# First and fourth attention: rounded upper halves of queries and keys on ScalarE, lower halves on VectorE, both from PSUM

## The chip, the cores and the metric

The kernel runs on one core of one Trainium2 chip. Its time is the device time of one execution in microseconds (us). Engines: TensorE (PE, its weight loads PEld), VectorE (DVE), ScalarE (ACT), GpSimd (POOL), SyncE (SP, which issues nearly all DMAs).

## What is computed

Four layers on x, 16 batches of 112 tokens with 256 features. Each adds a cross-attention with a context of 375 rows a batch, and then a feed-forward part (three mixtures of experts and a dense one). The change concerns the attentions of layer 0 and layer 3, which have 16 heads of 16 features:

```python
qh = (q @ W_q.T + b_q)...;  kh = (k @ W_k.T + b_k)...;  vh = (v @ W_v.T + b_v)...   # q = layernorm(x), k = v = ctx
scores = einsum('bhqd,bhkd->bhqk', qh, kh) / sqrt(16)
scores = where(mask == 0, -inf, scores)          # layer 3: -1e9
x = x + softmax(scores) @ vh ... @ W_o.T + b_o   # layer 3: the same without biases
```

The mask drops the same keys for all heads and queries.

## The kernel before

One program holds the instruction streams of the five engines; they meet at semaphores only. An attention is a list of steps, `Att.steps`, that PE, DVE and ACT each walk in the same order, each taking its own part of a step. The list is made of **slots**, one for each head: 256 for the 16 batches of an attention with 16 heads, plus a tail. In slot g stand, in this order: in slot 5 of a batch the `norm` step of the batch before (DVE: reciprocals of the sums and their spreading, L1146 and L1149); `scores` of head g (PE L918, then the DVE row minimum L1169, which adds the mask and writes the sum to SBUF; ACT's exponential of it, L1217, comes with a later step); `turn` of head g-3 (PE transposes, L935; the copy out of PSUM is DVE's, L1190, for three heads of eight, and ACT's, L1224, for the others), after which ACT takes the exponential of head g; in every fourth slot `pv` (PE L966); in slot 5 a transpose of the reciprocals (PE L871, ACT L1258, DVE L1060, which multiplies them in); and last the slot's "extras", which are the projections.

The projections of batch b+1 are spread over the 16 slots of batch b by `spread`. Each item has a cost; its slot is the first slot of the batch plus 15 times the share of the cost done before it, and never earlier than the item before it. For the output projection `o` of batch b-1 the rule also asks for at least one slot after the item before it, and for slot 7 or later: `max(first + int(done / total * count), earliest, last + (step is o))`. In a steady batch the queries q come in slot 0, key tile k0 in slot 1, k1 in slot 4, o in slot 8, the three value tiles in slots 9, 11 and 13. Two marks of cost 0 stand among the keys: `split` 0 (slot 1, ahead of k0), `split` 1 (slot 4, ahead of the next item) and `split` 2 (slot 7). Projections use PSUM banks 5, 6 and 7 in turn; projection n waits until projection n-3 is read out.

The score matmul of a head is one pass in the F32R format, over 128 rows that stack four 32-row pieces: products of rounded upper and rounding-error lower halves of queries and keys. They are made so: DVE reads the queries from PSUM and multiplies them by a 0/-0.25 pattern, once for each parity of heads (L1076 in layer 0, with bias; L1079 in layer 3), 2 x 224 columns; ACT reads a key tile from PSUM (L1247, L1249); `split` then runs on DVE from SBUF to SBUF: a rounding copy (L1049) and a subtraction (L1051). The halves go to DRAM ("spill", SP L1290 for queries, L1293 for keys) and come back rearranged ("stack": `qS` by four DMAs L1299, `kS` by four DMAs L1303 for each key tile). Scores of slots 0 to 7 need the first key tile's stack, those of slots 8 to 15 the second one's. SP issues in order: query spill, k0 spill, 4 query stacks, 4 k0 stacks, k1 spill, 4 k1 stacks, a context load.

Of the kernel before, what the change touches and what calls it, by code (L numbers as in the profile page):

```python
# [24 lines left out]
F32 = mybir.dt.float32  # L25
# [85 lines left out]
class Att:  # L111
# [4 lines left out]
    def __init__(self, L, sems, before):  # L116
# [30 lines left out]
        if self.stack:  # L147
            self.spilled = sems[f"spilled{L}"]
            self.split = sems[f"split{L}"]
            self.stacked, self.stacked8 = sems[f"stacked{L}"], sems[f"stacked8{L}"]  # L150
# [30 lines left out]

    def proj(self, b):
# [5 lines left out]
        if self.stack:  # L188
            return q + [(("split", b, 0), 0, 0), k[0], (("split", b, 1), 0, 0), k[1], (("split", b, 2), 0, 0)], v
        return ([(("ctx", b), 0, 0)] if self.halves else []) + q + k, v  # L190
# [27 lines left out]
    def steps(self):  # L218
# [7 lines left out]
        def spread(items, first, count):  # L226
# [18 lines left out]
        if H > 1:  # L245
            a, c = self.proj(0)
            ahead = [s for s, _, _ in a + c]
            for b in range(B):
# [214 lines left out]
def build(nc, A):  # L463
    ctx = ExitStack()
    with ctx:
# [8 lines left out]
        sel16 = sb("sel16", [P, 8])  # L474
# [42 lines left out]
        sel2 = sb("sel2", [P, 2])  # L517
# [3 lines left out]
        keys = wflat[:, 0:6 * SKE].rearrange("p (k o t) -> p k o t", k=3, o=2)  # L521
        queries = wflat[:, 6 * SKE:6 * SKE + 12 * S].rearrange("p (k o t) -> p k o t", k=3, o=2)
        STACK = 32
        NSTACK = P // STACK
        STACK_DMAS = [2 * NSTACK * 16, NSTACK * 16]
# [52 lines left out]
        for L in (0, 3):  # L578
            att_sems[f"spilled{L}"] = [sem(f"l{L}a_spilled{k}") for k in range(3)]
            att_sems[f"stacked8{L}"] = [sem(f"l{L}a_stacked8{k}") for k in range(2)]  # L580
            att_sems[f"split{L}"] = sem(f"l{L}a_halves")
            att_sems[f"stacked{L}"] = [sem(f"l{L}a_stacked{k}") for k in range(2)]
        att_sems["halved"] = sem("l2a_halved")
        folded_ps, folded_sb = sem("l1a_folded_psum"), sem("l1a_folded_sbuf")
# [62 lines left out]
        qhalves = nc.dram_tensor("query_halves", (2, 2 * P, 2 * S), F32).ap()  # L647
# [330 lines left out]
        def att_vector(dve, t):  # L978
            L, H, dh, per = t.L, t.H, t.dh, t.per
            n_chain = t.ch0  # L980
            if t.masked:
# [3 lines left out]
                dve.tensor_scalar(maskf[:, :], m[:, :], 0.0, t.a["fill"], ALU.is_equal, ALU.mult)\  # L985
# [27 lines left out]
            if t.stack:  # L1013
                dve.memset(keys[:, 0, :, SK:SKE], 0.0).then_inc(t.chain, 1)
# [23 lines left out]
            def split(b, part):  # L1038

                a = queries if part == 0 else keys[:, :, part - 1:part, :]  # L1040
                if part == 0:
                    freed(dve, t, t.gen_index("q", b, 0))
                else:
                    freed(dve, t, t.gen_index("k", b, part - 1))
                at = b * 6 + part * 2
                if part and b:
                    former, n = (t.stacked8, STACK_DMAS[1]) if part == 2 else (t.stacked, STACK_DMAS[0])
                    dve.wait_ge(former[(b - 1) % 2], n * ((b - 1) // 2 + 1))
                dve.tensor_copy(a[:, 1].bitcast(F32R), a[:, 0]).then_inc(t.split, 1)  # L1049
                dve.wait_ge(t.split, at + 1)  # L1050
                dve.tensor_tensor(a[:, 2].bitcast(F32R), a[:, 0], a[:, 1], ALU.subtract).then_inc(t.split, 1)  # L1051

            def gen(kind, b, o, h, n):
# [10 lines left out]
                if kind in "kn" or (kind == "v" and not t.a["bv"]) or (kind == "q" and H == 1):  # L1064
                    return
                dve.wait_ge(t.gen_ready, t.g0 + n + 1)
                if kind == "q" and t.stack:

                    if b:
                        dve.wait_ge(t.stacked[(b - 1) % 2], STACK_DMAS[0] * ((b - 1) // 2 + 1))  # L1070
                    by_parity = sel2[:, :].unsqueeze(2).broadcast_to([P, 2, S])
                    for j in range(t.NO):
                        out = queries[:, 0, j, :].rearrange("p (e s) -> p e s", e=2)
                        q2 = src[:, j * S:(j + 1) * S].unsqueeze(1).broadcast_to([P, 2, S])
                        if t.a["bq"]:
                            ins = dve.scalar_tensor_tensor(out=out, in0=q2, scalar=biasA[:, 0, j:j + 1],  # L1076
                                                           in1=by_parity, op0=ALU.add, op1=ALU.mult)
                        else:
                            ins = dve.tensor_tensor(out, q2, by_parity, ALU.mult)  # L1079
                elif kind == "q":  # L1080
# [79 lines left out]
            for s in t.plan:  # L1160
                if s[0] == "gen":
                    gen(*s[1:])
                elif s[0] == "scores":
# [19 lines left out]
                elif s[0] == "turn":  # L1183
# [6 lines left out]
                    dve.tensor_copy(pTb(t, g), bank[2 + g % 2][0:KT, 0:NKT * S]).then_inc(t.pt_sbuf[1], 1)  # L1190
                elif s[0] == "ctx":
                    halve_context(s[1])
                elif s[0] == "split":
                    split(s[1], s[2])
# [7 lines left out]
        def att_scalar(act, t):  # L1202
# [29 lines left out]

            def gen(kind, b, o, h, n):
                if kind in "or" or (kind == "q" and H > 1) or (kind == "v" and t.a["bv"]):
                    return
                src = bank[t.banks[n % t.GB]]
                act.wait_ge(t.gen_ready, t.g0 + n + 1)
                if kind == "q":
                    ins = act.activation(qall[:, o, b * S:b * S + TOK], src[:, 0:TOK], ACT.Identity,
                                         bias=folded[:, o:o + 1], scale=-t.a["scale"])  # L1240
                elif kind == "k":
                    out = keys[:, 0, o, 0:SK] if t.stack else kTv(t, b)[:, o, :]
                    if t.stack and b:
                        former, m = (t.stacked8, STACK_DMAS[1]) if o else (t.stacked, STACK_DMAS[0])
                        act.wait_ge(former[(b - 1) % 2], m * ((b - 1) // 2 + 1))
                    if t.a["bk"]:
                        ins = act.activation(out, src[:, 0:SK], ACT.Identity, bias=biasA[:, 1, o:o + 1])  # L1247
                    else:
                        ins = act.activation(out, src[:, 0:SK], ACT.Copy)  # L1249
                elif kind == "v" and t.stack:  # L1250
                    if b == 0 and o == 0:
                        act.wait_ge(padded, 2)
# [25 lines left out]
        def stack_sync(sp, t):  # L1278
# [4 lines left out]
            def batch(b):  # L1283
# [5 lines left out]
                sp.wait_ge(t.split, b * 6 + 2)  # L1289
                sp.dma_start(spill(qhalves), queries[:, 1:3]).then_inc(t.spilled[0], 16)  # L1290
                for o in range(2):
                    sp.wait_ge(t.split, b * 6 + 4 + o * 2)
                    sp.dma_start(spill(khalves[o]), keys[:, 1:3, o:o + 1, :]).then_inc(t.spilled[1 + o], 16)  # L1293
                    if o == 0:
                        if b >= 2:
                            sp.wait_ge(t.scores, t.h0 + (b - 1) * t.H)
                        sp.wait_ge(t.spilled[0], b * 16 + 16)
# [3 lines left out]
                    sp.wait_ge(t.spilled[1 + o], b * 16 + 16)  # L1301
# [860 lines left out]
        def _(pool):  # L2162
            pool.memset(part(V_AT, 2 * VPAD, KT), 0.0).then_inc(padded, 1)
            nc.gpsimd.iota(lanei[:, :], pattern=[[1, P]], base=0, channel_multiplier=0).then_inc(consts, 1)
# [4 lines left out]
            nc.gpsimd.memset(sel16[:, :], -ATT[0]["scale"]).then_inc(consts, 1)  # L2169
# [159 lines left out]
```

## Time and profile before

| what | value |
|---|---|
| median of 3 runs | 2513.31 us (2509.89 to 2515.79) |
| the profiled execution's own time | 2517.43 us |
| its span in the trace | 2515.4 us |
| layer 0 attention, first score to last pv | about 50 to 386 us |
| layer 3 attention, first score to last pv | about 2063 to 2391 us |
| busy over the span | PE 90%, PEld 69%, DVE 50%, ACT 42%, POOL 12% |

A row of the timeline has start, length, engine, line, operation, output<-input, shape and count; in square brackets the engine's idle time just before and who ended it. "mx" is the row minimum that the score needs, bank is PSUM, arena is one large SBUF tile that holds most buffers. In the chain of waits a row has start, length, what. Lines are those of the kernel before.

### The profile page before, as it was taken

Reading aid. Unit: us, or ns where it says so; the run is one execution under the profiler, and the core shown is the slowest. Engines: PE = TensorE matmul, PEld = TensorE weight load, DVE = VectorE, ACT = ScalarE, POOL = GpSimd, SP = SyncE. Lnnn points to the kernel's source line nnn. Section 1 sums busy time; section 2 is a strip of 40 time slices with the busy share of each in tenths; the row PEclk is TensorE's granted clock in tenths of the full one; section 3 lists DMA queues with packets and bytes.
Section 4 is the critical chain, followed back from the end, with each engine's and each line's share of the span. In section 5 each row is a group of like instructions: output and inputs, shape, how many; then the busy total and the mean of one; then the engine's idle time right before and its main releaser. Section 6 shows DMA issues by size and latency. Waiting matters only on the chain.

```text
span 2515.4 us, 44690 instructions
## 1 busy us (share of the span) xinstructions
PE 2254.5 (90%) x15374; PEld 1737.6 (69%) x15374; DVE 1254.1 (50%) x3592; ACT 1048.3 (42%) x2821; POOL 300.1 (12%) x349
## 2 busy tenths in 40 slices
PE   4999998999967899679999999999869949999998
PEld 3777776677746667467777777777547637777755
DVE  5777884222243522544445444454432267777713
ACT  2777772222132122134444444444312227877811
POOL 0000001111151245100000000000024300000020
PEclk8999998999978799889999999999869969999999
DMA  6887875222254212310000000000042168888600
GB/s 187 204 199 198 200 173 238 84 84 86 82 146 153 112 61 72 73 53 10 14 7 17 11 17 7 11 17 1 17 189 65 59 183 203 200 199 201 148 11 22
DMA packets 149433, 252.53 MB, mean 100 GB/s; under 512 B 14736, under 2 KB 124640, under 8 KB 146544
## 3 DMA queue, kind: packets, MB, share of 16 engines
q1 hardware_dynamic: 138560, 220.31, 32.4%
q0 software_dynamic: 10656, 29.37, 3.6%
q8 instruction: 131, 2.15, 0.4%
q14 instruction: 86, 0.70, 0.1%
HBM read 191.04 MB, written 58.59 MB: 99 GB/s over the span
## 4 chain that ended last, share of the span: by engine, by line
PE 76%; DVE 12%; DMA 5%; issue 4%; ACT 1%; SPq 1%; DVEq 0%; POOL 0%; ACTq 0%; POOLq 0%
PE bank L1676 8%; PE bank L935 7%; PE bank L966 6%; PE bank L1709 6%; PE bank L854 5%; PE bank L850 5%; PE bank L1741 5%; PE bank L880 4%; PE bank L923 4%; PE bank L865 3%; PE bank L841 3%; PE bank L1726 3%; PE bank L918 2%; PE bank L2034 2%; PE bank L2020 2%
## 5 line engine op out<-in xcount | busy, mean ns | idle before, releaser
L935 PE MATMUL bank<-ident,arena 112*125 112x112 f32 x2352 | 371.7, 275 | 3.3 <-DVE arena L1190 0.3
L935 PEld LDWEIGHTS bank<-ident,arena 112*125 112x125 f32 x2352 | 338.1, 188 | 46.5 <-issue 12.3
L1217 ACT ACTIVATE arena<-arena,mx 112x375 f32<-112x375 f32 x512 | 308.6, 604 | 116.5 <-DVE mx L1169 115.8
L1169 DVE CUSTOM_DVE_ANT_0 arena<-bank,maskf 112x375 f32<-112x375 f32 x512 | 273.3, 542 | 80.7 <-PE bank L918 79.1
L918 PE MATMUL bank<-kS,qS 128*112 128x376 f32 x512 | 236.4, 462 | 47.1 <-DMA kS<-key_halves 23.5
L1181 DVE TENSOR_REDUCE mx<-bank 112x1 f32<-112x375 f32 x256 | 128.8, 543 | 239.6 <-PE bank L923 239.5
L1676 PE MATMUL bank<-arena 128*128 x532 | 229.9, 555 | 3.4 <-ACT arena L1802 2.7
L1190 DVE COPY arena<-bank 125x336 f32<-125x336 f32 x448 | 214.2, 502 | 33.6 <-PE bank L935 33.6
L1217 ACT ACTIVATE arena<-bank,mx 112x375 f32<-112x375 f32 x272 | 156.0, 575 | 171.5 <-DVE mx L1181 150.1
L966 PE MATMUL bank<-arena 125*32 125x112 f32 (+1 forms) x4608 | 202.5, 265 | 2.9 <-DVE arena L1190 2.9
L966 PEld LDWEIGHTS bank<-arena 125*32 125x32 f32 (+1 forms) x4608 | 144.2, 118 | 85.6 <-issue 67.9
L1320 POOL TENSOR_TENSOR rstd<-newton,root 112x2 f32<-112x2 f32 x32 | 22.7, 709 | 1483.0 <-DVE newton L1125 1482.9
L1224 ACT ACTIVATE arena<-bank 125x336 f32<-125x336 f32 x336 | 147.0, 438 | 58.9 <-PE bank L935 55.9
L1709 PE MATMUL bank<-arena 128*128 (+1 forms) x672 | 167.1, 380 | 0.0
L850 PE MATMUL bank<-ctx_halves,weight_halves 128*128 128x376 f32 x768 | 144.8, 341 | 9.7 <-DVE arena L1082 9.7
L854 PE MATMUL bank<-weight_halves,ctx_halves 128*126 128x512 f32 x576 | 148.5, 403 | 0.0
L1676 PEld LDWEIGHTS bank<-arena 128*128 128x128 f32 x532 | 99.6, 191 | 66.0 <-issue 47.0
L1741 PE MATMUL bank<-xnT,arena 128*128 128x224 f32 (+1 forms) x640 | 143.2, 369 | 0.3 <-DVEq L658 0.3
L850 PEld LDWEIGHTS bank<-ctx_halves,weight_halves 128*128 128x128 f32 x768 | 131.4, 190 | 9.8 <-DVE arena L1082 9.8
L918 PEld LDWEIGHTS bank<-kS,qS 128*112 128x112 f32 x512 | 91.0, 178 | 68.1 <-issue 29.7
L1598 POOL DMA_INDIRECT results<-arena,scatter_id x91 | 89.9, 988 | 361.0 <-ACT arena L1824 281.9
L1741 PEld LDWEIGHTS bank<-xnT,arena 128*128 128x128 f32 (+1 forms) x640 | 111.8, 181 | 24.9 <-issue 11.6
(245 smaller groups left out, 3461.8 us busy)
## 6 DMA issues: line engine op xcount, KB each, us to landing
kS<-key_halves SPq DMA_DIRECT2D x256, 188.0 KB, 5.5
qS<-query_halves SPq DMA_DIRECT2D x128, 224.0 KB, 4.4
arena<-in_ctxT SPq DMA_DIRECT2D x64, 376.0 KB, 5.0
key_halves<-arena SPq DMA_DIRECT2D x64, 376.0 KB, 5.2
arena<-in_f_out SPq DMA_DIRECT2D x21, 768.0 KB, 4.5
query_halves<-arena SPq DMA_DIRECT2D x32, 448.0 KB, 4.0
arena<-in_f_up SPq DMA_DIRECT2D x4, 2816.0 KB
arena<-results SPq DMA_DIRECT2D x20, 448.0 KB, 7.9
```

What stands on the lines that cost most here:

```text
L850: m = pe.matmul(dst[:, 0:SKE], wH[:, 0, wh, c * t.W + o * P:c * t.W + (o + 1) * P], ctxH[:, ch, c, :], **flags)
L854: m = pe.matmul(dst[0:KT + 1, 0:t.VW], ctxH[:, ch, c, o * KT:(o + 1) * KT + 1], wH[:, 1, wh, c * t.W + h * t.VW:c * t.W + (h + 1) * t.VW], ...
L918: m = pe.matmul(bank[g % 2][0:S, 0:SKE], qS[:, b % 2, h * S:(h + 1) * S].bitcast(F32R), kS[:, b % 2, h // 2 * SKE:(h // 2 + 1) * SKE].bitc ...
L935: m = pe.transpose(bank[2 + g % 2][0:KT, k * S:(k + 1) * S], pr[:, g % t.NR, k * KT:(k + 1) * KT], ident[0:S, 0:S])
L966: m = pe.matmul(out, v, pTv(t, g + j)[:, k, :], **flags)
L1169: dve.tensor_tensor_reduce(sm[:, g % 2, :], bank[g % 2][0:S, 0:SK], maskf[:, :], 1.0, 3e38, ALU.add, ALU.min, mx[:, g % t.NR:g % t.NR + 1])\
L1190: dve.tensor_copy(pTb(t, g), bank[2 + g % 2][0:KT, 0:NKT * S]).then_inc(t.pt_sbuf[1], 1)
L1217: act.activation(pr[:, g % t.NR, :], src, ACT.Exp, bias=mx[:, g % t.NR:g % t.NR + 1], scale=-1.0, accum_out=row_sum(t, b)[:, h:h + 1]).the ...
L1224: act.activation(pTb(t, g), bank[2 + g % 2][0:KT, 0:NKT * S], ACT.Copy).then_inc(t.pt_sbuf[0], 1)
L1676: ins = pe.matmul(bank[m % 2][:, 0:w * f.NU], xTb(n)[:, k, :], up[:, bass.ds(expert[n], 1), at:at + w * f.NU].rearrange("p e n -> p (e n)" ...
L1709: ins = pe.matmul(bank[4 + n % 2][:, 0:D], midT_of(f, m)[:, j * P:(j + 1) * P], w2, start=(q + j == 0), stop=(q == G - 1 and j == J - 1))
L1741: ins = pe.matmul(bank[f.hidden_bank[s]][0:w, u * 2 * S:(u + 1) * 2 * S], up[u][:, k, o:o + w], xnT[:, k, c * 2 * S:(c + 1) * 2 * S], star ...
```

## The change

Queries and keys of layers 0 and 3:

- ACT reads a projection from PSUM and writes the rounded upper half at once (`upper_half`), queries included. Queries are no longer scaled or doubled by parity: 224 columns (in layer 0 two instructions of 112, for the bias). The scale and its sign go into the mask's minimum (L1169) as its factor.
- DVE makes the lower half by one subtraction, PSUM less upper half (`lower_half`; queries in layer 0 two of 112 columns), and it is DVE's instruction that frees the bank. The step `lower` is put in the extras of the slot after the projection's. The `split` marks are gone from the list that `spread` walks.
- The query spill has half the bytes (rows of 448 B where they were 896 B). The query stack is 8 DMAs to 16 partitions each, where it was 4 to 32; the other parity's columns stay zero, from a GpSimd memset of `qS` (128 x 3584) at the start and again ahead of layer 3.
- ACT's wait before it overwrites a half is for the former spill, not the former stack. SP waits for the former stack before it spills.
- The constants sel16 and sel2 are gone.

```diff
-            self.split = sems[f"split{L}"]
...
         if self.stack:
-            return q + [(("split", b, 0), 0, 0), k[0], (("split", b, 1), 0, 0), k[1], (("split", b, 2), 0, 0)], v
...
                 extras[slot].append(step)
+                if self.stack and step[1] in ("q", "k"):
+                    extras[slot + 1].append(("lower", step[2], 0 if step[1] == "q" else 1 + step[3]))
                 last = slot
...
-            def split(b, part):
-
-                a = queries if part == 0 else keys[:, :, part - 1:part, :]
...
-                dve.tensor_copy(a[:, 1].bitcast(F32R), a[:, 0]).then_inc(t.split, 1)
-                dve.wait_ge(t.split, at + 1)
-                dve.tensor_tensor(a[:, 2].bitcast(F32R), a[:, 0], a[:, 1], ALU.subtract).then_inc(t.split, 1)
+            def lower_half(b, part):
+
+                n = t.gen_index("k", b, part - 1) if part else t.gen_index("q", b, 0)
+                src, free = bank[t.banks[n % t.GB]], t.gen_free[n % t.GB]
+                dve.wait_ge(t.upper, t.half_at(b, part))
...
+                elif part == 0:
+                    ins = dve.tensor_tensor(queries[:, 1, :, :].bitcast(F32R),
+                                            src[:, 0:2 * S].rearrange("p (o t) -> p o t", t=S), queries[:, 0, :, :],
+                                            ALU.subtract)
+                elif t.a["bk"]:
+                    ins = dve.scalar_tensor_tensor(out=keys[:, 1, part - 1, 0:SK].bitcast(F32R), in0=src[:, 0:SK],
+                                                   scalar=biasA[:, 1, part - 1:part], in1=keys[:, 0, part - 1, 0:SK],
+                                                   op0=ALU.add, op1=ALU.subtract)
                 else:
...
+                    ins = dve.tensor_tensor(keys[:, 1, part - 1, 0:SK].bitcast(F32R), src[:, 0:SK],
+                                            keys[:, 0, part - 1, 0:SK], ALU.subtract)
+                ins.then_inc(free, 1)
...
                         dve.tensor_tensor_reduce(sm[:, g % 2, :], bank[g % 2][0:S, 0:SK], maskf[:, :],
-                                                 1.0, 3e38, ALU.add, ALU.min, mx[:, g % t.NR:g % t.NR + 1])\
+                                                 -t.a["scale"], 3e38, ALU.add, ALU.min, mx[:, g % t.NR:g % t.NR + 1])\
...
+            def upper_half(b, part, src):
+
+                if b:
+                    act.wait_ge(t.spilled[part], t.s0 + 16 * b)
...
+                elif part == 0:
+                    ins = act.activation(queries[:, 0, :, :].bitcast(F32R),
+                                         src[:, 0:2 * S].rearrange("p (o t) -> p o t", t=S), ACT.Copy)
...
+                ins.then_inc(t.upper, 1)
...
-                sp.wait_ge(t.split, b * 6 + 2)
-                sp.dma_start(spill(qhalves), queries[:, 1:3]).then_inc(t.spilled[0], 16)
+                if b:
+                    sp.wait_ge(t.stacked[(b - 1) % 2], STACK_DMAS[0] * ((b - 1) // 2 + 1))
+                freed(sp, t, t.gen_index("q", b, 0))
+                sp.dma_start(spill(qhalves), queries[:, :]).then_inc(t.spilled[0], 16)
...
                         for part_ in range(NSTACK):
-                            sp.dma_start(to_q[part_ * STACK:(part_ + 1) * STACK],
-                                         qhalves[part_ // 2].rearrange(pairs, r=STACK)).then_inc(t.stacked[p], 16)
...
+                            for e in range(2):
+                                row = part_ * STACK + e * 16
+                                sp.dma_start(to_q[row:row + 16, :, e * S:(e + 1) * S],
+                                             qhalves[part_ // 2].rearrange("(g e r) t -> e r g t", e=2, r=16)[e])\
+                                    .then_inc(t.stacked[p], 16)
...
             pool.memset(part(V_AT, 2 * VPAD, KT), 0.0).then_inc(padded, 1)
+            pool.memset(qS[:, :, :], 0.0).then_inc(padded, 1)
```

## Rows read from the trace of the kernel before

**Rows 1.** Busy time by window: PE, PEld, DVE, ACT, POOL; clock, DMA share, GB/s.
```profile
200.00:300.00 100.00, 93.67 (x933) 78.40 (x926) 79.98 (x271) 72.95 (x213) 2.82 (x4) 1.00 0.83 200
```
**Rows 2.** Who waited for whom (us, times, longest): PE, 50 to 120 us, then 2060 to 2370 us.
```profile
PE bank L918 <- DMA kS<-key_halves: 13.3, 3, 10.9
...
PE bank L918 <- DVE mx L1169: 11.4, 14, 0.9
...
PE bank L918 <- DMA kS<-key_halves: 10.1, 2, 8.1
```
**Rows 3.** Timeline of slots 2 to 8 of one steady batch in layer 0.
```profile
203.06 0.50 DVE L1190 COPY arena<-bank 125x336 f32<-125x336 f32 x1
...
204.91 0.34 DVE L1049 CAST arena<-arena 128x376 fp32r<-128x376 f32 x1
...
205.29 0.55 DVE L1051 TENSOR_TENSOR arena<-arena 128x376 fp32r<-128x376 f32 x1
...
205.57 0.57 ACT L1247 ACTIVATE arena<-bank,biasA 128x375 f32<-128x375 f32 x1 [0.18 <-PE bank L861]
...
206.31 0.54 DVE L1169 CUSTOM_DVE_ANT_0 arena<-bank,maskf 112x375 f32<-112x375 f32 x1
...
206.89 0.61 ACT L1217 ACTIVATE arena<-arena,mx 112x375 f32<-112x375 f32 x1 [0.39 <-DVE mx L1169]
...
207.50 0.34 ACT L1258 ACTIVATE oT<-bank 128x224 f32<-128x224 f32 x1
...
207.87 0.39 DVE L1060 TENSOR_TENSOR oT<-bank,oT 128x224 f32<-128x224 f32 x1 [1.01 <-ACT oT L1258]
208.17 0.54 DVE L1169 CUSTOM_DVE_ANT_0 arena<-bank,maskf 112x375 f32<-112x375 f32 x1
...
208.87 0.40 PE L918 MATMUL bank<-kS,qS 128*112 128x376 f32 x1 [0.81 <-DVE mx L1169]
...
209.42 1.03 PE L880 MATMUL bank<-arena,oT 128*112 128x256 f32 x4
```
**Rows 4.** Instructions grouped by line: count, busy us, mean ns, idle before them.
```profile
L1076 DVE SCALAR_TENSOR_TENSOR arena<-bank,biasA,sel 128x224 f32<-128x224 f32 x24 | 9.7, 446 | 6.1 <-PE bank L841 6.1
...
L1096 DVE TENSOR_TENSOR x<-bank,x 112x256 f32<-112x256 f32 x14 | 5.9, 420 | 0.0
...
L1079 DVE TENSOR_TENSOR arena<-bank,sel 128x224 f32<-128x224 f32 x30 | 10.3, 386 | 8.2 <-PE bank L841 8.2
```
**Rows 5.** The chain of waits, start of layer 0 and of layer 3.
```profile
0.82 11.33 DMA x<-in_x
...
35.83 0.82 DVE arena L1076 x2
...
37.76 2.81 DMA query_halves<-arena
...
43.88 6.55 DMA kS<-key_halves
...
2056.69 6.71 DMA kS<-key_halves
```
**Rows 6.** SP's DMA issues at the start of layer 0.
```profile
40.58 1.82 SPq L1299 DMA_DIRECT2D qS<-query_halves  x4
42.44 1.87 SPq L1303 DMA_DIRECT2D kS<-key_halves  x4
...
58.79 0.36 SPq L1293 DMA_DIRECT2D key_halves<-arena  x1
...
61.99 1.87 SPq L1303 DMA_DIRECT2D kS<-key_halves  x4
```
**Rows 7.** DMA queue q1 in 46.5 to 50.4 us, then 62 to 65 us: packets, MB, share.
```profile
q1 hardware_dynamic: 686, 0.94, 108.5%
...
q1 hardware_dynamic: 786, 0.66, 114.8%
```
**Rows 8.** GpSimd's clearing of the value pads ahead of layer 3.
```profile
2033.68 2.66 POOL L2200 MEMSET arena<- 125x3072 f32 x1 [25.35 <-DVEq L658]
```

More of the change, by code:

```diff
@@ L180, in head, with half_at @@
         return i
+    def half_at(self, b, part):
+        return self.u0 + b * 3 + part + 1
     def proj(self, b):
@@ L247, in steps @@
             ahead = [s for s, _, _ in a + c]
+            if self.stack:
+                ahead[3:3] = [("lower", 0, part) for part in range(3)]
             for b in range(B):
@@ L578, in build @@
         for L in (0, 3):
-            att_sems[f"spilled{L}"] = [sem(f"l{L}a_spilled{k}") for k in range(3)]
             att_sems[f"stacked8{L}"] = [sem(f"l{L}a_stacked8{k}") for k in range(2)]
-            att_sems[f"split{L}"] = sem(f"l{L}a_halves")
             att_sems[f"stacked{L}"] = [sem(f"l{L}a_stacked{k}") for k in range(2)]
         att_sems["halved"] = sem("l2a_halved")
+        att_sems["spilled"] = [sem(f"halves_spilled{k}") for k in range(3)]
+        att_sems["upper"] = sem("upper_halves")
         folded_ps, folded_sb = sem("l1a_folded_psum"), sem("l1a_folded_sbuf")
@@ L1013, in att_vector @@
             if t.stack:
-                dve.memset(keys[:, 0, :, SK:SKE], 0.0).then_inc(t.chain, 1)
+                dve.memset(keys[:, :, :, SK:SKE], 0.0).then_inc(t.chain, 1)
                 n_chain += 1
@@ L1063, in gen @@
                     return
-                if kind in "kn" or (kind == "v" and not t.a["bv"]) or (kind == "q" and H == 1):
+                if kind in "kn" or (kind == "v" and not t.a["bv"]) or (kind == "q" and (H == 1 or t.stack)):
                     return
                 dve.wait_ge(t.gen_ready, t.g0 + n + 1)
[L1067 to L1080, printed above, removed]
+                if kind == "q":
                     ins = dve.tensor_scalar(qmv(t, b)[:, o:o + t.QG, :],
@@ L1190, in att_vector @@
                     dve.tensor_copy(pTb(t, g), bank[2 + g % 2][0:KT, 0:NKT * S]).then_inc(t.pt_sbuf[1], 1)
+                elif s[0] == "lower":
+                    lower_half(s[1], s[2])
                 elif s[0] == "ctx":
                     halve_context(s[1])
-                elif s[0] == "split":
-                    split(s[1], s[2])
                 elif s[0] == "norm":
@@ L1231, in summed_up @@
                     .then_inc(t.norm, 1)
+            def upper_half(b, part, src):
+                if b:
+                    act.wait_ge(t.spilled[part], t.s0 + 16 * b)
+                if part == 0 and t.a["bq"]:
+                    for j in range(2):
+                        ins = act.activation(queries[:, 0, j, :].bitcast(F32R), src[:, j * S:(j + 1) * S], ACT.Identity,
+                                             bias=biasA[:, 0, j:j + 1])
+                elif part == 0:
+                    ins = act.activation(queries[:, 0, :, :].bitcast(F32R),
+                                         src[:, 0:2 * S].rearrange("p (o t) -> p o t", t=S), ACT.Copy)
+                elif t.a["bk"]:
+                    ins = act.activation(keys[:, 0, part - 1, 0:SK].bitcast(F32R), src[:, 0:SK], ACT.Identity,
+                                         bias=biasA[:, 1, part - 1:part])
+                else:
+                    ins = act.activation(keys[:, 0, part - 1, 0:SK].bitcast(F32R), src[:, 0:SK], ACT.Copy)
+                ins.then_inc(t.upper, 1)
             def gen(kind, b, o, h, n):
-                if kind in "or" or (kind == "q" and H > 1) or (kind == "v" and t.a["bv"]):
+                if kind in "or" or (kind == "q" and H > 1 and not t.stack) or (kind == "v" and t.a["bv"]):
                     return
@@ L1237, in gen @@
                 act.wait_ge(t.gen_ready, t.g0 + n + 1)
+                if kind in "qk" and t.stack:
+                    upper_half(b, 0 if kind == "q" else 1 + o, src)
+                    return
                 if kind == "q":
@@ L1241, in gen @@
                 elif kind == "k":
[L1242 to L1249, printed above, removed]
+                    ins = act.activation(kTv(t, b)[:, o, :], src[:, 0:SK], ACT.Copy)
                 elif kind == "v" and t.stack:
                     if b == 0 and o == 0:
-                        act.wait_ge(padded, 2)
+                        act.wait_ge(padded, 3)
                     ins = act.activation(pad_of(b, o), src[0:KT, 0:D].rearrange("p (j e d) -> p j e d", e=2, d=16), ACT.Copy)
@@ L2200, in _ @@
                     pool.memset(part(V_AT, 2 * VPAD, KT), 0.0).then_inc(padded, 1)
+                    pool.memset(qS[:, :, :], 0.0).then_inc(padded, 1)
                     add_b2(pool, att[L], f)
```

58 lines of the change are left out of this document (25 added, 33 removed).

## The prediction, made before the changed kernel was run

> **What bounds the kernel now.** I read the busy time by window first, then who waited for whom, then the timeline of one batch, and last the chain of waits at each attention's start. In the steady stage of an attention PE is busy 93.67 of 100 us, DVE 80, ACT 73, and the DMA engines carry a share of 0.83 [rows 1]. So PE bounds it, and a relieved DVE is worth only what PE waits for DVE. That wait is one event a batch: 11.4 us in 14 waits, 0.81 us each [rows 2]. The timeline shows its place: the score of slot 8 starts at 208.87 after 0.81 us idle, released by the row minimum of slot 6, which DVE began at 208.17 [rows 3]. Outside the steady stage PE waits for the stacks: in layer 0 13.3 us, 10.9 before the first score and 2.4 at the next two batches; in layer 3 10.1, of which 8.1 and 2.0 [rows 2].
>
> **DVE between slots 2 and 8.** An instruction's successor starts some 0.09 us before its recorded end (L1060 at 207.87 for 0.39, successor at 208.17) [rows 3], so I count lengths less 0.08. Split 1 goes: 204.91 to 205.84 less 0.08, 0.85 us [rows 3]. A subtraction from PSUM takes 386 ns for 224 columns and 420 for 256 [rows 4], 1.06 ns a column, so 0.55 for 375. With the bias it is 446 ns for 224 [rows 4], so 0.61. Counted: 0.47 in layer 3, 0.53 in layer 0. There are two key subtractions a batch and both now come earlier: the one of k0 in slot 2 (split 1 was in slot 4), that of k1 in slot 5 (split 2 was in slot 7, behind the critical minimum).
> Layer 0, followed through: after the copy at 203.06 comes the new subtraction, so the minima of slots 3 and 4 move back by 0.5. ACT's exponentials follow them, and its readout of k1 moves from 205.57 to about 205.8. Split 1's 0.85 is gone, so the minimum of slot 5 moves forward from 206.31 to 206.0. ACT is then the later one: its exponential moves from 206.89 to about 206.6, L1258 from 207.50 to 207.2, L1060 from 207.87 to 207.6. Now k1's subtraction stands ahead of the critical minimum, which starts at 207.6 + 0.30 + 0.53 = 208.4, where it was 208.17. Taken alone this makes PE's wait **longer** by 0.24 us a batch in layer 0, and by some 0.14 in layer 3.
>
> **The output projection moves.** `spread` puts o at the latest of its share, slot 7 and one slot behind the item before it. That item was split 2 in slot 7, hence slot 8. With the marks gone it is k1 in slot 4, the share is 3.42/6.86 x 15 = 7.5, and o falls into slot 7, ahead of the score of slot 8 on PE. It is 1.03 us of PE work [rows 3] and needs only L1060, which ends at 207.98. PE has nothing left from 208.06 (208.87 less 0.81). So o starts at about 208.1 and runs to 209.15, and by then the minimum of slot 6 is done (208.4 + 0.55 = 208.96). The gap of 0.81 shrinks to about 0.07. New: DVE's copy of slot 7 (0.50 long, as L1190 [rows 3]) ends at 208.4 + 0.47 + 0.47 + 0.50, about 209.85, and PE's transpose in slot 9 waits for it until 209.99, where it could start at 209.7: 0.28. Gain a batch in layer 0: 0.81 - 0.07 - 0.28 = 0.46. In layer 3 both subtractions are 0.06 shorter and ACT's readout is too: I take 0.60. The 14 batches 1 to 14 have projections and an o: 14 x 0.46 + 14 x 0.60 = **14.8 us**.
>
> **Query work.** DVE loses in slots 0 and 1 two L1076 (0.82 us [rows 5]) and a copy and subtraction of 448 columns (to 37.76 in the same place at the start, 1.1 us [rows 5]), and gets about 0.6. PE does not wait there, so this is worth nothing in the steady stage. ACT gains an instruction of 224 columns, as L1258's 0.34 [rows 3], or two of 112; it idles before the next minimum, so I count nothing, and 0.2 a batch if that cover is gone. The banks: value tile 0 needs k1's bank, which DVE now frees at 208.5, over 1 us before PE comes to it.
>
> **DMAs.** The counts of packets stay: 512 for the query spill, 1024 for the query stack; bytes halve. Two windows in which the queue is full give 108.5% x 3.9 us x 16 / 686 = 99 ns for a mean packet of 1370 B and 114.8% x 3 x 16 / 786 = 70 ns for 840 B [rows 7]: 73 ns at 896 B, and by the same line 49 ns at 448 B. Bounds: 49 and 73 (no gain); no row has a large number of 448 B packets. I take 49, since two rows lie on that line. SP issues four more DMAs a batch, 0.46 us each (1.82 for 4 [rows 6]): 1.85 us later for the k0 stack. In the steady stage both are hidden, as no PE wait there is for a stack.
>
> **Starts.** Layer 0: DVE's query work begins at 35.83 and ends at 37.76; now two subtractions of 112, 0.6 us, so the spill leaves 1.3 earlier. It lands 2.81 later as before or sooner, at 39.3; 8 stack issues to 43.05, k0's to 44.9, 1.0 later than 43.9. But the landing was queue bound: 1024 x 73 + 512 x 106 ns (k0 stack, 1504 B) + 256 x 106 (k1 spill) over 16 engines is 9.8 us from 40.6, and it came at 43.88 + 6.55 = 50.43 [rows 5, 6]. Now the query part (3.1 us) runs within its issue time, then 3.4 + 1.7 from 43.1 on, and one latency: about 48.5. Gain 1.9. Layer 3: its k0 spill is only 0.4 earlier and SP's issue later, the landing was 6.71 after the last issue [rows 5]: gain 1.2. Batch 1 in both: k0's half is ready 1.8 earlier than 58.79, SP's eight query issues use that up (k0 stack again at about 62 [rows 6]), but the queue is shorter by 1.5 us and more: the wait of 2.0 goes in both layers, and layer 0's further 0.4. Sum 1.9 + 1.2 + 2.4 + 2.0 = **7.5 us**; from both sides 2 and 10.
> GpSimd's memset of qS is 3584/3072 x 2.66 = 3.1 us [rows 8]. At the start the constants end that much later, at about 10, and DVE's first work waits for x until 12.15 [rows 5]: nothing. Ahead of layer 3 it runs to 2039.4, the first query stack is ten us later: nothing.
>
> **Sum.** Against the profiled execution's own 2517.4: 2517.4 - 14.8 - 7.5 = 2495.1. The median of the runs is 4.1 lower, so I predict **2491** for it.
>
> **Rivals.**
> (A) *The gap is not filled.* o can only start when L1060 is done, and L1060 waits for ACT, which has the queries' halves as new work and exponentials held back by 0.5. If L1060 comes 0.5 later than I have it, o starts as late as the score did and what is left is the longer DVE chain: 14 x 0.24 + 14 x 0.14 = 5 lost, 3 to 7.5 won at the starts: 2509 to 2515, about 2511. For it: ACT is busy 73 of 100. Against: it idled 0.18 and 0.39 in this stretch [rows 3].
> (B) *The small packets cost more, not less* (slower). Place: the DMA queue in every batch. The share of 0.83 [rows 1] of a batch's 20.2 us leaves 3.4 us x 16 / 1536 = 36 ns a query packet. Below 73 + 36 = 109 ns nothing happens, above it the queue sets the batch. At twice today's price, 146 ns, it is 1536 x 73 / 16 = 7.0 us more, 3.6 over, 28 batches: +100 us, 2610.
> The Trainium skill ("DMA: Bandwidth & Descriptors", Specifications) speaks against the change here: it asks for transfers of at least 512 B and says that below this the DMA engine does a read-modify-write. By it the sum would go from the gain above to (B), if that costs a second pass; no row here tells, the trace has no stage of such packets.
> (C) *VectorE waits for ScalarE's halves with score minima queued behind* (slower). Place: slot 2, where DVE comes to k0's subtraction at 203.5 and ACT's half is done at about 203.0 (0.57 after PE's product). Margin 0.5; each further delay goes into the minima of slots 3 to 6. Beyond 1.4 us of delay the 0.46 and more is lost; at 2 us, a batch is 0.5 longer and the whole 2520.
>
> **Chances.** Forecast 0.70 (own range 2481 to 2503); A 0.20, half of it faster by over 0.2%; B 0.05; C 0.05. About 0.2%, 5 us, is what a measurement can tell from no change. Low end: the full 0.81 in 28 batches and 10 at the starts, 2513.3 - 33 = 2481. High end: a gain of 0.1 a batch and 3 at the starts, 2507, which leaves out half of A, B and C. Faster 0.80, same 0.10, slower 0.10.
>
> **What would show it.** L880 ahead of the slot 8 score on PE and no 0.8 us wait there, but a short one at the next transposes; the minimum of slot 6 some 0.24 later; PE's waits for kS down to some 9 and 7 us; DMA share near 0.75; DVE's busy time some 55 us down, ACT's some 12 up. A DMA share at or over 0.9 in the steady stage would mean B; a DVE wait for L1247's successor, C; L1060 at or after its old place, A.

## The result, and the profile after

The median of the changed kernel is 2490.65 us (2489.17 to 2493.27), that of the kernel before, measured beside it, 2511.60: ratio 0.9916, 95% interval 0.9898 to 0.9933. A second measurement on another chip gave 2489.73 against 2508.74, ratio 0.993 (0.9917 to 0.9942). The forecast was 2491. The profiled execution took 2493.27 us, its span 2491.5, that of before 2515.4.

The page of the kernel after, engine busy times and the lines that changed (columns as in the page of before: busy us and mean ns behind the first bar, idle time of the engine before them behind the second):

```profile
PE 2263.3 (91%) x15374; PEld 1737.3 (70%) x15374; DVE 1197.5 (48%) x3447; ACT 1054.6 (42%) x2869; POOL 305.2 (12%) x348
...
L923 PE MATMUL bank<-kS,qS 128*112 128x376 f32 x512 | 232.9, 456 | 19.0 <-DMA kS<-key_halves 18.2
```

DVE did 1254.1 us of work before and does 57 less; ACT did 1048.3 and does 6 more. The score matmuls (L923, formerly L918) have 19.0 us of idle time before them, where they had 47.1.

The window of [rows 1] in the kernel after:

```profile
200.00:300.00 100.00, 97.72 (x981) 80.18 (x979) 73.10 (x257) 76.91 (x233) 2.81 (x4) 1.00 0.67 173
```

PE is busy 97.7 of 100 us where it was 93.7, DVE 73.1 where it was 80.0, and the DMA share is 0.67 where it was 0.83.

Who PE waited for in the kernel after; 50 to 120 us, 100 to 380 us, then 2020 to 2370 us (us in total, times, longest):

```profile
PE bank L923 <- DMA kS<-key_halves: 1.7, 1, 1.7
...
PE bank L892 <- DVE xn L1136: 5.7, 7, 0.8
...
PE bank L923 <- DMA kS<-key_halves: 7.8, 2, 7.4
```

The wait for the row minimum is gone from both lists. Its row in [rows 2], 11.4 us in 14 waits, is that of layer 3; layer 0 of the kernel before has it too, 0.82 us each, in 110 to 360 us:

```profile
PE bank L918 <- DVE mx L1169: 9.9, 12, 1.0
```

What PE waits for most in the steady stage is now the transposes of a layernorm (L892, 7 batches, up to 0.8 us).

The timeline of one steady batch, slots 2 to 8. The copy of slot 2 starts at 198.06 here and at 203.06 in [rows 3], so 5.00 is to be added to compare the two:

```profile
197.41 0.57 ACT L1245 ACTIVATE arena<-bank,biasA 128x375 fp32r<-128x375 f32 x1 [1.62 <-PE bank L866]
...
198.06 0.50 DVE L1190 COPY arena<-bank 125x336 f32<-125x336 f32 x1
...
198.48 0.60 DVE L1058 SCALAR_TENSOR_TENSOR arena<-bank,biasA,arena 128x375 fp32r<-128x375 f32 x1
...
200.77 0.55 ACT L1245 ACTIVATE arena<-bank,biasA 128x375 fp32r<-128x375 f32 x1
200.89 0.54 DVE L1169 CUSTOM_DVE_ANT_0 arena<-bank,maskf 112x375 f32<-112x375 f32 x1
...
202.15 0.35 ACT L1272 ACTIVATE oT<-bank 128x224 f32<-128x224 f32 x1
...
202.53 0.39 DVE L1073 TENSOR_TENSOR oT<-bank,oT 128x224 f32<-128x224 f32 x1 [1.09 <-ACT oT L1272]
...
202.84 0.60 DVE L1058 SCALAR_TENSOR_TENSOR arena<-bank,biasA,arena 128x375 fp32r<-128x375 f32 x1
...
203.06 1.09 PE L885 MATMUL bank<-arena,oT 128*112 128x256 f32 x4
...
203.35 0.54 DVE L1169 CUSTOM_DVE_ANT_0 arena<-bank,maskf 112x375 f32<-112x375 f32 x1
...
204.04 0.41 PE L923 MATMUL bank<-kS,qS 128*112 128x376 f32 x1
...
204.28 0.51 DVE L1190 COPY arena<-bank 125x336 f32<-125x336 f32 x1
...
204.93 0.55 PE L940 MATMUL bank<-ident,arena 112*125 112x112 f32 x3
```

The reader is to see three things. The output projection (L885, formerly L880) stands ahead of the score of slot 8 (L923 at 204.04), and PE begins it at 208.06 on the old scale, where the gap of 0.81 us began. The two subtractions (L1058) come at once behind what precedes them, so DVE finds ACT's half (L1245, done at 197.98) ready. The minimum of slot 6 (L1169 at 203.35, 208.35 on the old scale) is 0.18 later than before and costs PE next to nothing, because the projection lies above it.

How much is left of the wait shows in the chain of waits over the same stretch (start, length, what):

```profile
203.06 1.09 PE bank L885 x4
204.15 0.30 PE bank L923
204.45 0.32 PE bank L940 x3
204.77 0.17 PE bank L923
204.94 0.54 PE bank L940 x3
```

A score takes 0.17 of the chain and its transposes 0.32 where nothing holds them. The score of slot 8 took 0.30 and the transposes of slot 9 took 0.54: 0.13 and 0.22 us are lost there, in place of 0.81.

**The period of a batch.** Measured on DVE's reciprocal (L1146, once a batch), two steady batches together (mean of six such pairs), and from the landing of x to the first score of layer 0, in us:

| kernel | two batches, layer 0 | two batches, layer 3 | x to first score |
|---|---|---|---|
| before | 42.47 | 41.27 | 38.33 |
| before, second profile | 42.49 | 41.29 | 38.34 |
| after | 41.56 | 40.23 | 35.90 |
| after, second profile | 41.55 | 40.23 | 35.39 |

A batch is 0.46 us shorter in layer 0 and 0.52 in layer 3. This mean repeats to 0.02 us between executions, so it is a much sharper measure of the steady stage than the whole time.

### The profile page after: what moved, and what is told of

Same layout as the page of the kernel before. It is cut to its first block, busy times and chain, and to the rows that moved or that the text cites. A ratio compares the mean times of both kernels' runs of the same rounds, so it can differ in the third digit from the quotient of the medians.

```text
span 2491.5 us, 44722 instructions
## 1 busy us (share of the span) xinstructions
PE 2263.3 (91%) x15374; PEld 1737.3 (70%) x15374; DVE 1197.5 (48%) x3447; ACT 1054.6 (42%) x2869; POOL 305.2 (12%) x348
## 4 chain that ended last, share of the span: by engine, by line
PE 81%; DVE 9%; DMA 4%; SPq 2%; issue 2%; ACT 1%; POOL 0%; DVEq 0%; another core or an unknown queue 0%; ACTq 0%; POOLq 0%
PE bank L940 10%; PE bank L1699 8%; PE bank L971 7%; PE bank L1732 6%; PE bank L855 5%; PE bank L859 5%; PE bank L1764 5%; PE bank L885 4%; PE bank L928 4%; PE bank L923 3%; PE bank L870 3%; PE bank L846 3%; PE bank L866 3%; PE bank L1749 3%; PE bank L2057 2%
## 5 line engine op out<-in xcount | busy, mean ns | idle before, releaser
L1169 DVE CUSTOM_DVE_ANT_0 arena<-bank,maskf 112x375 f32<-112x375 f32 x512 | 270.0, 543 | 128.8 <-PE bank L923 127.7
L923 PE MATMUL bank<-kS,qS 128*112 128x376 f32 x512 | 232.9, 456 | 19.0 <-DMA kS<-key_halves 18.2
L1699 PEld LDWEIGHTS bank<-arena 128*128 128x128 f32 x532 | 99.7, 191 | 66.4 <-issue 47.4
L1732 PEld LDWEIGHTS bank<-arena 128*128 128x128 f32 x672 | 117.5, 190 | 10.6
```

Of the source, the lines that this page charges most:

```text
L923: m = pe.matmul(bank[g % 2][0:S, 0:SKE], qS[:, b % 2, h * S:(h + 1) * S].bitcast(F32R), kS[:, b % 2, h // 2 * SKE:(h // 2 + 1) * SKE].bitc ...
L1699: ins = pe.matmul(bank[m % 2][:, 0:w * f.NU], xTb(n)[:, k, :], up[:, bass.ds(expert[n], 1), at:at + w * f.NU].rearrange("p e n -> p (e n)" ...
L1732: ins = pe.matmul(bank[4 + n % 2][:, 0:D], midT_of(f, m)[:, j * P:(j + 1) * P], w2, start=(q + j == 0), stop=(q == G - 1 and j == J - 1))
```

## The experiments

The theory: the steady gain comes from one thing, the output projection that slid from slot 8 to slot 7 and fills the gap in front of the score of slot 8. DVE's lighter load alone brings nothing there, since its chain to the critical minimum got longer. The rest of the gain is at the starts. The rival: the gain is DVE's relief (57 us less work), and the place of the projection is a side effect.

**The change again, as a yardstick.**

> The changed kernel again, as the reference for its neighbours on the same chip. Theory (order: the output projection fills PE's gap): 2491 us, 0.991 of the kernel before; two batches of layer 0 take 41.5 us and of layer 3 40.2 us, as in its first profile (before: 42.4 and 41.3). If the 5 us that the middle of the program gave (layer 2's experts, not touched by the change) were luck of the granted clock, this profile may lack them and the time be up to 2496.

Measured: 2489.73 us, 0.993 (0.9917 to 0.9942). It is the time against which the next three are held. The four behind them ran on another chip, where the kernel before took 2510.72 us; they are compared by their ratio to it and by their periods.

**The change, with the output projection held in slot 8.** In `spread`, behind the expression for the slot:

```diff
+                if self.stack and step[:2] == ("gen", "o") and slot == first + 7:
+                    slot += 1
```

> The changed kernel, but with the output projection of the batch before back in slot 8 (layers 0 and 3); all else as changed. Theory (order): the gap ahead of the slot 8 score is back and longer than it was before the change, about 1.0 us in layer 0 (the subtraction of key tile 1 stands ahead of the critical minimum) and 0.95 in layer 3; a batch costs 0.6 to 0.7 us more than in the changed kernel, 28 batches 17 to 20 us: 2508 to 2511, about the time of the kernel before less what the starts give. Rival (relief: VectorE's 57 us less work is what pays, the order is nothing): no change against the changed kernel, 2491.

Measured: 2507.22 us, 0.9996 (0.9986 to 1.0006). PE's waits in 110 to 360 us:

```profile
PE bank L925 <- DVE mx L1171: 11.8, 12, 1.0
PE bank L894 <- DVE xn L1138: 4.9, 6, 0.8
```

The wait for the minimum is back, and it is longer than in the kernel before: 11.8 / 12 = 0.98 us each against 0.81. Two batches take 42.79 and 41.45 us, 0.16 and 0.09 a batch more than before. So the change without the move loses in the steady stage, as the theory said (0.24 and 0.14), 14 x 0.16 + 14 x 0.09 = 3.5 us, and the starts give that back. The rival falls: DVE's relief is all there (it is busy for 1201.0 us, before for 1254.1) and the time is that of before.

**The kernel before, with the output projection moved to slot 7.** The other half of the pair:

```diff
+                if self.stack and step[:2] == ("gen", "o") and slot == first + 8:
+                    slot -= 1
```

> The kernel before, but with the output projection in slot 7 (layers 0 and 3); halves still made by split on VectorE, all DMAs as before. Theory (order): the projection starts at the end of its multiplication (208.3 in the batch shown) and fills 0.81 less 0.1 to 0.25 of the gap: 0.55 to 0.7 a batch, 28 batches 15 to 20 us: 2492 to 2497. Rival (relief): no gain, 2512.

Measured: 2495.82 us, 0.9952 (0.9939 to 0.9965), two batches 41.67 and 40.38 us. PE's waits in 110 to 360 us:

```profile
PE bank L889 <- DVE xn L1138: 4.9, 6, 0.8
PE bank L882 <- DVE oT L1062: 4.4, 12, 0.5
```

The wait for the minimum is gone here too. In its place the projection itself waits for its input (DVE's product L1062, formerly L1060), 0.37 us each. In one steady batch of layer 0 DVE begins the product 1.92 us behind the start of PE's pv in slot 5 (206.00 less 204.08), in the kernel after 1.58 us behind it (202.53 less 200.95). Split 1 (0.85 us), which still stands in DVE's way in slot 4, accounts for it by the order of the steps; no run takes it out alone. The four medians side by side, all against the same runs of before:

| | projection in slot 8 | projection in slot 7 |
|---|---|---|
| halves as before | 2508.74 | 2495.82 |
| halves as after | 2507.22 | 2489.73 |

The move alone brings 12.9 us, both changes 19.0. The new halves alone bring 1.5, which their interval can't tell from none. The remaining 4.6 are the two together: in the kernel after the projection finds its input ready. The periods say the same of the steady stage, in us a pair of batches in layer 0 and layer 3: the move alone 0.80 and 0.89 less, the halves alone 0.32 and 0.18 more, both 0.92 and 1.04 less.

**The lower half of k1 two slots later.** If 0.13 and 0.22 us remain because k1's subtraction stands ahead of the critical minimum, they should go when it stands behind it (slot 7 in place of slot 5):

```diff
-                    extras[slot + 1].append(("lower", step[2], 0 if step[1] == "q" else 1 + step[3]))
+                    late = 3 if step[1] == "k" and step[3] == 1 and slot == first + 4 else 1
+                    extras[slot + late].append(("lower", step[2], 0 if step[1] == "q" else 1 + step[3]))
```

> The changed kernel, but in a steady batch VectorE's subtraction for key tile 1 comes in slot 7 (behind that slot's copy out of PSUM) in place of slot 5. Theory: the minima of slots 6 and 7 and the copy of slot 7 come 0.5 us earlier, so PE's transpose in slot 9 no longer waits 0.22 us for the copy: 28 x 0.2 = 6 us, 2485; key tile 1's spill leaves 1 us later and stays hidden. Rival: the wait moves to the next thing (the multiplication L1073, which starts the projection), and the gain is under 2 us.

Measured: 2480.78 us, 0.989 (0.9875 to 0.9904), more than I expected. Two batches take 40.79 and 39.61, so 0.38 and 0.31 less a batch than after. The chain of waits at the same place of a batch:

```profile
198.63 1.09 PE bank L886 x4
199.72 0.17 PE bank L924
199.89 0.32 PE bank L941 x3
200.21 0.18 PE bank L924
200.39 0.32 PE bank L941 x3
```

Score and transposes are back at 0.17 and 0.32: both losses are gone, 0.35 together. I had counted the second alone. So what limited the changed kernel at this place was the new subtraction ahead of the minimum of slot 6.

**More small packets.** The queries' spill is written three more times, to DRAM that nothing reads; the next batch's ACT write waits for these transfers, so that they take part in the order. It adds 3 x 512 packets of 448 B a batch, as many again as the change's own small ones:

```diff
+                    if o:
+                        for copy in range(3):
+                            sp.dma_start(spill(unread[copy]), queries[:, :]).then_inc(unread_done[copy], 16)
```

> The changed kernel with three more spills of the query halves a batch in layers 0 and 3, to DRAM tensors that nothing reads: 1536 more packets of 448 B, twice the query packets, issued behind key tile 1's spill. Theory (small packets are cheap: 605 of them in 2 us at a share of 59.3% are 31 ns each): 1536 x 31 / 16 = 3.0 us more DMA work in a batch of 20.4, the share goes from 0.67 to about 0.82, and the steady batches take the same 41.6 and 40.2 us a pair; only the starts lose, 0 to 4 us: 2490 to 2495. Rival (packets under 512 B cost a second pass once the queue is loaded, 100 ns and more): share over 1, pairs 10 us longer, over 2600.

Measured: 2492.82 us, 0.9929 (0.9906 to 0.9951); two batches 41.53 and 40.21, as in the kernel after. Queue q1 in 110 to 360 us (packets, MB, share of 16 engines), first of after, then of this kernel, and this kernel's window of [rows 1]:

```profile
q1 hardware_dynamic: 42168, 40.31, 63.1%
```
```profile
q1 hardware_dynamic: 61528, 49.06, 79.5%
...
200.00:300.00 100.00, 97.66 (x980) 80.12 (x979) 72.77 (x256) 76.91 (x232) 2.81 (x4) 1.00 0.83 206
```

16.4% more of 250 us on 16 engines, over 19360 packets, is 34 ns each. The DMA share is back at the 0.83 of before, and no time is lost: these transfers are covered in the steady stage. It bears only on rival (B), which needed over 109 ns a packet.

**Queries' second half behind the first keys.** At a start PE waits for the first key stack and the query stack. The edit puts the last four of the eight query issues behind the four of k0, so that the keys start earlier:

```diff
-                        for part_ in range(NSTACK):
+                        for part_ in range(2):
...
+                    for part_ in range(2, NSTACK if o == 0 else 2):
```

> The changed kernel with SP's order four query stacks, four stacks of key tile 0, four query stacks, in place of eight and four. Theory (the start waits for the key stack, which is the long transfer and stands behind eight short ones): the last landing comes 1 to 1.5 us earlier at the first score of each layer, and PE's wait at batch 1 in layer 0 (1.7 us) goes: 2 to 4 us, 2486 to 2488. Rival (the key spill's landing holds SP back by as much): no change, 2490.

Measured: 2486.34 us, 0.9905 (0.9885 to 0.9925). Inconclusive: the interval overlaps that of the kernel after. The first score comes 35.73 us after x, where the two profiles of after have 35.90 and 35.39. PE's wait at the start of layer 3, 7.4 us for the keys, is now one for the queries:

```profile
PE bank L923 <- DMA qS<-query_halves: 7.1, 1, 7.1
```

The kernel leaves this edit little to win. The last four query issues fill rows 64 to 127 of `qS`, and every score reads all 128 rows; PE also waits with one count for all twelve landings (`stacked`, 3 x 4 x 16). So in both orders the stack that lands last sets the start, and the order decides only which one that is. At batch 1 of layer 0 a wait of 0.6 us is left (after: 1.7 in one profile, none in the other).

**Both edits together.** The later lower half of k1 and the divided query stack in one kernel.

> Both the later subtraction for key tile 1 (slot 7) and SP's order with the key stack in between. If the two act in different stages, they add up: 2480.8 less 2 to 4, 2477 to 2479.

Measured: 2478.20 us, 0.9872 (0.9853 to 0.9891); two batches 40.81 and 39.61, first score 35.79 us after x, PE's wait for the queries in layer 3 7.3. The steady part repeats to 0.02 us; the part at the starts can't be told from none, here too.

**The next wait.** In the kernel after, and with the later subtraction as well, PE's longest steady wait is that of the layernorm's transposes (L892, L893 with the later subtraction) for DVE's output xn, up to 0.8 us in 6 of the batches of layer 0. `follow` lays the steps of the layernorm into one slot after the other; the edit gives these transposes one slot more, on top of the later subtraction:

```diff
-                at += 2 if step[1] == "r" else 1
+                at += (2 if step[1] == "r" else 1) if not self.stack or b == B - 1 else 2 if step[1] == "n" else 1
```

> The kernel with the later subtraction for key tile 1, and in layers 0 and 3 PE's transposes of the normalised rows (L892, every second batch) one slot later, so that PE has a score and its transposes before them. PE waits there for VectorE's rows 0.8 us in layer 0 and 0.6 in layer 3. Theory (any PE work that needs nothing fills such a gap): 7 x 0.7 + 7 x 0.5 = 8 us, 2472. Rival (the wait only moves to the router's matmul one slot later, which needs ScalarE's copy of these transposes): under 2 us, 2480.

Measured: 2473.80 us, 0.9854 (0.9836 to 0.9871), two batches 40.30 and 39.11. PE's waits in 110 to 360 us, first with the later subtraction alone, then with this edit too, and this kernel's window 200 to 300 us:

```profile
PE bank L893 <- DVE xn L1137: 4.9, 6, 0.8
...
PE bank L886 <- DVE oT L1074: 0.5, 1, 0.5
```
```profile
PE bank L924 <- DVE mx L1170: 1.0, 6, 0.2
PE bank L886 <- DVE oT L1074: 0.5, 1, 0.5
PE bank L900 <- ACT xnT L1275: 0.4, 1, 0.4
...
200.00:300.00 100.00, 98.92 (x997) 82.73 (x997) 75.09 (x265) 79.34 (x237) 2.81 (x4) 1.00 0.69 174
```

The 4.9 us of waits for xn turn into 1.0 for the minimum and 0.4 for ScalarE's copy; the last, one wait of 0.4, is the one that the rival named. PE is busy 98.9 of 100 us. Two batches take 0.49 and 0.50 us less than with the later subtraction alone, 7 x 0.99 = 6.9 us where 8 were expected. It is the fastest kernel here, 36.9 us below before on its chip (2510.72), where the kernel after was 19.0 below before on the other.

**The kernel before, profiled again.** To see how far an untouched stretch varies by itself.

> The kernel before, profiled once more. Theory (the 5 us that the changed kernel's profile was shorter between layer 0's router and layer 3's first rows is chance of the granted clock, not the change): that stretch is again between 1620 and 1627 us, as in six profiles of other kernels, where the first profile of the kernel before had 1630; pairs of steady batches are 42.5 and 41.3 us as there. Rival (the change shortens the middle): 1630 again.

Measured: 2513.69 us, one run. From the last reciprocal of layer 0 (L1146) to the first instruction that adds layer 2's results to x (L1995, in after L2018) it took 1625.0 us; the first profile of before has 1630.2, the two of after 1625.0 and 1626.2, and the seven profiles of the other kernels 1619.8 to 1624.3. The periods of the table above repeat to 0.02 us.

The time came out as expected, the cause did not. In the two profiles of before PE's busy time in this stretch is 1494.7 and 1495.8 us and its granted clock 0.94 in both. What differs is waits: 3.0 us at one load of context rows, here in the first profile and then in the second (386 to 2015.6 and 387.2 to 2011.6 us), and 2.0 us at L850, which waits for DVE's L1082 (9.7 and 7.7).

```profile
PE bank L926 <- DMA arena<-in_ctxN: 12.0, 1, 12.0
```
```profile
PE bank L926 <- DMA arena<-in_ctxN: 9.0, 1, 9.0
```

Among the other profiles PE's busy time for this same work varies as well, from 1486.9 us at a clock of 0.95 to 1497.9 at 0.94.

## Why the prediction was right

The two profiled spans differ by 23.9 us. By stage: x landed 0.5 earlier (11.65 against 12.15, before the change can act); layer 0 from x to the router behind it 8.05; the middle, which the change doesn't touch, 5.15; layer 3 9.28; the end 0.9. The middle of before and of after (windows as in [rows 1]; the points of the stage sum lie some us inside them):

```profile
388.00:2016.00 1628.00, 1493.31 (x8606) 1123.67 (x8604) 658.13 (x1588) 503.00 (x1264) 251.17 (x282) 0.94 0.20 66
```
```profile
380.00:2002.00 1622.00, 1493.77 (x8604) 1125.10 (x8602) 659.01 (x1587) 502.90 (x1264) 250.60 (x282) 0.94 0.20 66
```

PE's work is the same to 0.5 us, and the second profile of before has the middle as short as after. So these 5 us are not the change but longer waits in the first profile of before (above); why that load took longer there is open.

The second profiles of both kernels, taken at the same places, give another split of 22.5 us between their spans: x 0.4 earlier, layer 0 11.75, the middle 0.6 longer in after, layer 3 10.1, the end 0.8. So the two attentions brought 8.05 + 9.28 = 17.3 us in one pair of profiles and 21.9 in the other, where I forecast 14.8 + 7.5 = 22.3. The medians differ by 21.0 and 19.0 us in the two measurements. The mechanism was right and the sum somewhat high. That 2491 was met to 0.4 us is partly luck: it was reckoned from a median of before of 2513.3, and the one measured beside the changed kernel is 2511.60, from which the same sum gives 2489.3.

**The output projection moves: right, to its parts.** On the old scale ACT's readout of k1 came at 205.77 (forecast 205.8), the minimum of slot 5 at 205.89 (206.0), L1073 at 207.53 (207.6). The projection started at 208.06 (208.1), the minimum of slot 6 at 208.35 (208.4), the copy of slot 7 ended at 209.79 (209.85). The gap left at the score was 0.13 (0.07), the new one at slot 9's transposes 0.22 (0.28); together 0.35 of the 0.81, as forecast, and 0.46 us a batch gained. Layer 3 gave 0.52 where I took 0.60: that "both subtractions are 0.06 shorter and ACT's readout is too" was worth less than I put on it. Steady sum 14 x 0.46 + 14 x 0.52 = 13.7 us for 14.8. Without the move the change would have cost PE 0.16 and 0.09 a batch (forecast 0.24 and 0.14), shown by holding the projection in slot 8.

**DVE's chain: right.** The subtraction from PSUM with bias took 598 ns (estimate 0.61), the one without 540 (0.55). DVE's total fell by 57 us (55).

**ACT: half of what I counted.** It rose by 6 us, not 12, and stayed in time.

**Starts: right in place, one term mis-sized.** PE's waits for the stacks, in the first and the second profile of each kernel:

| place | before | after | forecast gain | gain |
|---|---|---|---|---|
| layer 0, first score | 10.9, 10.9 | 8.7, 7.5 | 1.9 | 2.2, 3.4 |
| layer 0, batches 1 and 2 | 2.4, 2.2 | 1.7, 0 | 2.4 | 0.7, 2.2 |
| layer 3, first score | 8.1, 8.4 | 7.4, 8.3 | 1.2 | 0.7, 0.1 |
| layer 3, batches 1 and 2 | 2.0, 2.4 | 0.4, 0 | 2.0 | 1.6, 2.4 |

Together 5.2 in the first pair and 8.1 in the second, for 7.5. Not all of it is time won: in the second pair 1.6 us come back as a longer wait for DVE's query half (L870, 3.1 us, where L865 has 1.5 in before), and in the first layer 0 gave back 0.9, as batch 1 ran with a lower clock behind its wait (below) and took 21.40 us, where before it took 20.55. The step of the sum that failed is "the wait of 2.0 goes in both layers": in layer 3 it nearly does, in layer 0 only half of it. What ended PE's wait at batch 1 of layer 0 shows in the chain of the kernel after, with SP's issues below it:

```profile
51.35 4.70 DMA query_halves<-arena
...
62.19 4.50 DMA kS<-key_halves
...
56.07 4.57 SPq L1321 DMA_DIRECT2D qS<-query_halves  x8
60.68 1.94 SPq L1326 DMA_DIRECT2D kS<-key_halves  x4
```

I had the queue as the limit and the eight issues as lying under k0's lead. But the query spill took 4.70 us to land behind batch 0's key stacks, where the first one took 2.29, and SP can only then begin the eight issues and after them those of k0. The spill's landing and the issues stand one behind the other. In the second profile of after the spill took as long (4.66), but the twelve issues took 5.54 us in place of 6.55: the second query issue takes 1.36 us here and 0.43 there. The wait was not there, and batch 0 took 18.07 us against 19.18. The four other profiles with this order of issues have the wait too, 0.7 to 1.5 us, and twelve issues in 6.2 to 7.1 us. So five of six executions have it, 1.1 us on average over the six where the sum had none. What stretches an issue is not shown.

**Small packets: right in direction, price too high.** At the first start (40.2 to 42.2 us) 605 packets of some 400 B took 59.3% of 2 us on 16 engines, 31 ns each, and the added ones 34 ns; my line gave 49. The DMA share came to 0.67, not 0.75. The two rows on which the line lies are from stretches in which the queue was full. Over 110 to 360 us the kernel before has the row below: 78 ns a packet at a mean of 1170 B, where the line gives 88. So part of the error is that a packet's time in a full queue was taken for its price.

```profile
q1 hardware_dynamic: 40549, 47.43, 78.6%
```

The Trainium skill ("DMA: Bandwidth & Descriptors", Specifications), by which transfers below 512 B bring a read-modify-write, is not borne out as a cost here: had it meant a second pass, (B) would have come, with 146 ns a packet and about 2610 us.

**The rivals.** (A), the gap not filled, didn't come: L1073 ran at 207.53 on the old scale, earlier than L1060's 207.87 [rows 3]. (B) fell by the packets' price. (C), DVE waiting for ACT's half, fell: in the timeline DVE comes to k0's subtraction 0.50 us after ACT's half is done, the margin of the forecast.

## What to carry to other kernels

When a schedule is a fixed order, an edit can win by what it lets slide: look first at which long independent instruction of the bound engine ends up in front of its one wait, and try that move by itself in both kernels. Relief of an engine that is not the bound has to reach the instruction that the bound engine waits for; here the relief alone was worth 1.5 us, not to be told from none, the place of one matmul group 12.9, and placing the new work behind the critical minimum about 9 more. Compare periods of steady stages, which repeat to 0.02 us, before reading a whole time that varies by several us in parts that no edit touches. And before the order of two transfers is changed, look at what their reader waits for: if it needs both, the order changes little.

## What was not expected of the hardware

**Packets of 448 B are cheap**: 31 to 34 ns each, by 78 ns at a mean of 1170 B in the kernel before, or 70 ns at 840 B and 99 ns at 1370 B where the queue was full [rows 7].

**Behind a short wait the clock is sometimes lower.** In the profiled execution of after, PE waited 1.69 us for the first key stack of batch 1 (66.73), and from 68.0 to 71.4 us its granted clock was the lower of the two levels, 1.2 GHz, though it was busy all the time. Windows 66 to 68 and 68 to 71.4 us of after, then of its second profile, which had no such wait:

```profile
66.00:68.00 2.00, 1.27 (x11) 1.27 (x12) 0.56 (x2) 0.70 (x4) 0.00 (x0) 1.00 0.26 92
68.00:71.40 3.40, 3.40 (x33) 2.65 (x32) 1.05 (x4) 2.18 (x7) 0.00 (x0) 0.51 0.75 182
```
```profile
66.00:68.00 2.00, 2.00 (x37) 1.78 (x35) 1.22 (x5) 2.00 (x8) 0.00 (x0) 1.00 0.32 74
68.00:71.40 3.40, 3.31 (x25) 2.49 (x18) 2.02 (x7) 2.32 (x7) 0.00 (x0) 1.00 0.96 207
```

Batch 1 took 21.40 us there and 19.85 in the second profile. A wait of this length does not always bring it. The kernel before waited 2.04 us up to 70.14 in its first profile and kept 1.00; in its second it waited 2.16 us up to 69.95 and had 0.56 in 71.4 to 75 us. Four other profiles with waits of 0.7 to 1.5 us at this place kept 1.00 from 66 to 72 us. That it was the wait that lowered the clock is not shown; it would take runs that lengthen this wait alone.
